# Projections of a two-layer conditioned transformer kernel in three fp32r products instead of plain fp32, with the second conditioning streamed among the weights and a new order

## The chip, the cores and the metric

The kernel runs on one core of one Trainium2 chip. The metric is the device time of one execution in microseconds (us), median of the runs shown. TensorE (PE) multiplies matrices, its weight loads are shown apart (PEld); VectorE is DVE, ScalarE is ACT, GpSimd is POOL, and SyncE (SP) issues all the DMAs here. Each engine works through its own list of instructions in order and waits on semaphores for the others.

## What is computed

Two transformer layers over x (4 sequences of 512 rows, 256 channels, 16 heads of 16 channels), each conditioned by cond_1024. Cut to what matters:

```python
# layer 0
ada = silu(cond) @ ada_w.T + ada_b                  # six vectors of 256 per sequence
h = ln(x) * (1 + s1) + sh1
q, k, v = split(h @ qkv_w.T + qkv_b)                # rope on q and k
attn = softmax(q k^T / 4);  o = attn @ v
x = x + (o @ proj_w.T + proj_b) * g1
h2 = ln(x) * (1 + s2) + sh2
x = x + (gelu(h2 @ fc1_w.T + fc1_b) @ fc2_w.T + fc2_b) * g2
# layer 1: the same with rmsnorm and a gated MLP, conditioned by a small network
t = swiglu(cond @ w_t1 + b_t1) @ w_t2 + b_t2
h = rmsnorm(x) * g1 * (1 + scale1) + shift1;  x = x + mha(h)
h = rmsnorm(x) * g2 * (1 + scale2) + shift2;  x = x + (a * silu(gate)) @ w_fo + b_fo
```

All of it is in fp32. The tolerance is that of fp32, so a product in the faster type fp32r, which keeps fewer bits of its operands, is only good enough if the operands are split in a high and a low part.

## The kernel before

A unit is one sequence in one layer; there are 8 (`UNITS`), worked through one behind the other, four of layer 0 and then four of layer 1. A unit's 16 heads go in four quads of four heads, 32 quads in all. The work of a quad: `peaks` (scores with queries on the partitions, of which DVE takes the row maximum), `top` (the maxima are turned and go by DMA into the operand), `scores` (keys on the partitions, with the maximum subtracted inside the product), the exponential on ACT (L1428), `values` (L920) and `output`. Beside the quads of unit u run the projection and MLP of unit u-1 (`post_pieces`) and the norm, query, key and value projection of unit u+1 (`pre_pieces`).

The order is written out by hand: each piece of work has a tick in the tables `FIRST_AT`, `PRE_AT`, `POST_AT`, `SPLIT_AT`, `LOAD_AT`, `QUAD_AT` (a quad is 112 ticks, `SQ`, a unit 448), all pieces are sorted by tick, and each engine issues its own in that order. PSUM has eight banks: `ps_o` for the values, `ps_b` for the MLP's second product, and a ring of six that all other products share; each use gets the bank whose last reader comes first in the order.

What the change touches:

- `q_and_k` (L858): one output chunk of 128 query or key channels for 512 rows, two products (k = 0, 1) with plain fp32 weights `wf` and rows `hf`. `v` (L871) and `project` (L959): one tile of 128 rows against 256 channels, two products. An fp32 product shows in the trace as two matmul instructions.
- `hf` holds the rows of the first norm (h1), then of the attention output (o), then of the second norm (h2), so each writer waits for the last reader of the one before. ACT writes it in `modulated` (L1383) and `channels` (L1452).
- The MLP is already in three products: DVE rounds h2 to `hh` (L1230), POOL subtracts to get `hl` (L1565), and `up` (L989) multiplies high by low, low by high, high by high. Its weights come in chunks of 128x512 by `load_w`, through three staging places in `mlp`; ACT rounds each (`split_w`, L1485) and DVE subtracts (L1269). `down` (L1006) does the same with the hidden values.
- Rope: ACT takes q and k out of PSUM into `raw` (`take`, L1399), DVE and POOL multiply and add into `turned`, ACT rounds it to `high` (L1409), POOL subtracts to get `low` (L1542), SP spills both to DRAM (L792, L795), and `fill` (L807) reads them back in the layout of the quads.
- Layer 1's conditioning: `t1` and `t2` come whole (0.5 and 1 MB) into places that are used later, and `net_1` (L1032) and `net_2` (L1047) multiply in the first stage, before and between the first peaks.
- The bias of v is added by DVE in `take_v` (L1141).

## Time and profile before

| | us |
|---|---|
| median of 3 runs | 815.72 |
| runs | 815.72, 809.18, 816.38 |
| the profiled execution, its own time | 818.03 |
| its span, first to last instruction | 816.1 |
| PE busy | 769.3 |
| DVE busy | 632.6 |
| ACT busy | 491.0 |
| POOL busy | 290.6 |
| mean granted TensorE clock | 0.962 |

The sums of busy time overlap between engines. A matmul's row shows its own duration, which for neighbours in the pipeline overlaps; the time that a matmul takes of PE is the distance to the start of the next.

### The profile page before, as it was taken

The numbers are of one execution on the slowest core, as the hardware profiler recorded it, in microseconds if no ns is written. First come the engines' busy times: TensorE is split into PE (matmuls) and PEld (weight loads), VectorE is DVE, ScalarE is ACT, GpSimd is POOL, SyncE is SP. The second block draws the span as 40 slices with busy tenths as digits, with TensorE's granted clock in tenths as the row PEclk, the third lists the DMA queues.
The fourth block names the chain that finished last, engine by engine and source line by source line (L and its number), as shares of the span: only waits on it lengthen the run. The fifth ranks groups of instructions, "written<-read, shape, count | busy, mean of one in ns | idle before, by whom it ended". The sixth has DMA issues, their size and how long they took to land.

```text
span 816.1 us, 14249 instructions
## 1 busy us (share of the span) xinstructions
PE 769.3 (94%) x4800; PEld 485.8 (60%) x4800; DVE 632.6 (78%) x1349; ACT 491.0 (60%) x1015; POOL 290.6 (36%) x263
## 2 busy tenths in 40 slices
PE   4999999999999999999999999999999999999496
PEld 3654334466645765566646664668547685776396
DVE  3377898879887897879888999978878879753354
ACT  1114785777657875587758777674666656556132
POOL 0321204534354526334364335332343223222334
PEclk9776999999999999899999999999999999999799
DMA  8475645511234015414322515630254212000000
GB/s 323 130 208 155 191 121 143 155 40 41 84 102 136 14 32 150 135 40 143 79 85 60 144 52 143 183 92 1 65 143 126 57 40 67 2 1 27 1 2 27
DMA packets 34153, 76.27 MB, mean 93 GB/s; under 512 B 4512, under 2 KB 9248, under 8 KB 33824
## 3 DMA queue, kind: packets, MB, share of 16 engines
q1 hardware_dynamic: 34080, 75.35, 32.7%
q8 instruction: 39, 0.64, 0.3%
q14 instruction: 34, 0.28, 0.1%
HBM read 39.42 MB, written 35.65 MB: 92 GB/s over the span
## 4 chain that ended last, share of the span: by engine, by line
PE 72%; DVE 13%; POOL 4%; issue 3%; DMA 3%; ACT 2%; SPq 1%; POOLq 0%; ACTq 0%; DVEq 0%
PE ring L989 17%; PE ps_o L920 11%; PE ps_b L1006 10%; PE ring L893 8%; DVE top L1178 7%; PE ring L906 7%; PE ring L858 7%; PE ring L871 3%; PE ring L959 3%; DMA qt<-top_t 2%; PE ring L931 1%; POOL sines L1531 1%; PE ring L840 1%; POOL hl L1565 1%; PE ring L1020 1%
## 5 line engine op out<-in xcount | busy, mean ns | idle before, releaser
L1178 DVE TENSOR_REDUCE top<-ring 128x1 f32<-128x512 f32 x512 | 321.5, 683 | 42.3 <-PE ring L906 40.7
L1428 ACT ACTIVATE pr<-ring 128x512 f32<-128x512 f32 x512 | 270.2, 605 | 67.0 <-PE ring L893 62.9
L1572 POOL TENSOR_TENSOR act_l<-mlp,act_h 128x256 fp32r<-128x256 f32 x128 | 101.7, 795 | 248.0 <-DVE act_h L1255 248.0
L920 PE MATMUL ps_o<-pr,va 128*17 128x512 f32 x1024 | 133.9, 606 | 0.2 <-ACT pr L1428 0.2
L906 PE MATMUL ring<-kt,qt 48*128 48x512 f32 x512 | 123.3, 459 | 4.5 <-ACT pr L1428 1.3
L893 PE MATMUL ring<-qt,kt 49*128 49x512 f32 x512 | 117.5, 455 | 4.7 <-DMA qt<-top_t 4.2
L1465 ACT ACTIVATE mlp<-ring,col 128x256 f32<-128x256 f32 x128 | 61.1, 477 | 85.5 <-PE ring L989 57.5
L893 PEld LDWEIGHTS ring<-qt,kt 49*128 49x128 f32 x512 | 51.9, 185 | 76.2 <-issue 51.5
L906 PEld LDWEIGHTS ring<-kt,qt 48*128 48x128 f32 x512 | 56.4, 190 | 68.7 <-issue 38.6
L989 PE MATMUL ring<-hh,wl 128*128 128x256 f32 x384 | 83.5, 300 | 6.0 <-issue 3.5
L989 PE MATMUL ring<-hh,wh 128*128 128x256 f32 x384 | 79.4, 289 | 0.0
L989 PE MATMUL ring<-hl,wh 128*128 128x256 f32 x384 | 79.3, 289 | 0.0
L1241 DVE SCALAR_TENSOR_TENSOR mlp<-mlp 128x256 f32<-128x256 f32 x128 | 58.3, 455 | 26.5 <-ACT mlp L1472 24.9
L1006 PE MATMUL ps_b<-wh,act_l 128*128 128x256 f32 x256 | 78.0, 305 | 0.9 <-POOL act_l L1572 0.8
L989 PEld LDWEIGHTS ring<-hh,wl 128*128 128x128 f32 x384 | 61.0, 196 | 22.0 <-issue 12.2
L1006 PE MATMUL ps_b<-wl,act_h 128*128 128x256 f32 x256 | 72.3, 282 | 0.0
L1006 PE MATMUL ps_b<-wh,act_h 128*128 128x256 f32 x256 | 72.2, 282 | 0.0
L1531 POOL TENSOR_TENSOR sines<-raw,trig 128x1024 f32<-128x1024 f32 x16 | 44.1, 2758 | 77.5 <-issue 45.9
L858 PE MATMUL ring<-hf,wf 128*128 128x512 f32 x128 | 67.9, 673 | 1.3 <-ACT hf L1383 1.3
L989 PEld LDWEIGHTS ring<-hh,wh 128*128 128x128 f32 x384 | 62.0, 199 | 0.0
L989 PEld LDWEIGHTS ring<-hl,wh 128*128 128x128 f32 x384 | 61.7, 198 | 0.0
L1561 POOL TENSOR_TENSOR xs<-xs,add 128x512 f32<-128x512 f32 x32 | 40.9, 1280 | 55.2 <-DVE add L1216 53.8
(86 smaller groups left out, 1035.0 us busy)
## 6 DMA issues: line engine op xcount, KB each, us to landing
scratch<-high SPq DMA_DIRECT2D x48, 512.0 KB, 5.1
qt<-scratch SPq DMA_DIRECT2D x64, 192.0 KB, 3.5
kt<-scratch SPq DMA_DIRECT2D x64, 192.0 KB, 4.4
scratch<-low SPq DMA_DIRECT2D x16, 512.0 KB, 5.9
mlp<-in_w_split SPq DMA_DIRECT2D x20, 256.0 KB, 3.5
xs<-in_x SPq DMA_DIRECT2D x4, 512.0 KB, 5.1
out_x<-xs SPq DMA_DIRECT2D x4, 512.0 KB, 2.9
pr<-in_w_ada SPq DMA_DIRECT2D x2, 512.0 KB, 6.3
```

What stands on the lines that cost most here:

```text
L858: last = nc.tensor.matmul(bank[:, :], w[:, k, c * P:(c + 1) * P], hf[:, k, :], start=(k == 0), stop=(k == KC - 1))
L893: nc.tensor.matmul(bank[:, :], kt[r:r + SHIFT + 1, n % NSLOT, h // 2, t * P:(t + 1) * P], qt[r:r + SHIFT + 1, n % NSLOT, h // 2, :], start ...
L906: nc.tensor.matmul(bank[:, :], qt[r:r + SHIFT, n % NSLOT, h // 2, t * P:(t + 1) * P], kt[r:r + SHIFT, n % NSLOT, h // 2, :], start=True, s ...
L920: last = nc.tensor.matmul(ps_o[32 * h:32 * h + HD + 1, :], va[:, u % 2, t, QUAD * g + h, :], pr[:, slot, :], start=(t == 0), stop=(t == T ...
L989: last = nc.tensor.matmul(bank[:, s * TH:(s + 1) * TH], wp[:, k, c:c + P], hp[:, k, half * TH:(half + 1) * TH], start=(n == 0), stop=(n == ...
L1006: last = nc.tensor.matmul(ps_b[:, s * C:(s + 1) * C], ap[:, at % 2, s * P:(s + 1) * P], wp[:, f, :], start=(f == 0 and s == 0 and n == 0), ...
L1178: nc.vector.tensor_reduce(top[:, n % 2, c:c + 1], bank[:, :], AX_X, ALU.max, negate=True).then_inc(free, 1)
L1241: step(nc.vector.scalar_tensor_tensor(val[at % 2], aux[at % 2], 1.0, val[at % 2], ALU.add, ALU.mult))
L1428: nc.scalar.activation(pr[:, at % NP, :], bank[:, :], ACT.Exp, scale=SCALE).then_inc(free, 1)
L1465: nc.scalar.activation(val[at % 2], src, ACT.Identity, bias=col[:, c:c + 1]).then_inc(val_in, 1)
L1531: nc.gpsimd.tensor_tensor(sines[:, :, :], raw[:, :, :], trig[:, 1, :].unsqueeze(1).to_broadcast([P, 2, L]), ALU.mult).then_inc(sin_in, 1)
L1572: nc.gpsimd.tensor_tensor(act_l[:, at % 2, :], src, act_h[:, at % 2, :].bitcast(F32), ALU.subtract).then_inc(act_l_in, 1)
```

## The change

- The query, key, value and output projections are done in three fp32r products: weights in a high and a low part (`qh`, `ql`), rows in `hh` and `hl`. Each output takes 6 matmul instructions in place of 4.
- ACT writes the high part itself and then the plain value: two activations per 128x512 where there was one, in `modulated` and `channels`. The subtraction is `rest` on POOL, for h1, o and h2 (on DVE for the very first unit). DVE's rounding of h2 goes. h2 has its own `hh2` and `hl2`, so the waits between h1, o and h2 are others.
- Four chunks of layer 0's projection weights come first through the staging places and are split; layer 1's four come late (`late_load`, `split_late`) through one place of their own.
- Layer 1's conditioning weights come as six chunks through the same staging places, between the projection chunks and the MLP's; `net_1` and `net_2` are moved behind the first scores.
- The bias of v is added in `channels` instead of `take_v`, which becomes a copy.
- `high` and `low` of the rope are written over `raw` and `sines`. So `take` and `sine` of the next pair wait until the spill of the last has landed; before, only `high` and `low` waited for it.
- All the tables of ticks are new.

```diff
-                    for k in range(KC):
-                        last = nc.tensor.matmul(bank[:, :], w[:, k, c * P:(c + 1) * P], hf[:, k, :],
-                                                start=(k == 0), stop=(k == KC - 1))
+                    for wp, hp in ((ql, hh), (qh, hh), (qh, hl)):
+                        for k in range(KC):
+                            if wp is ql:
+                                pe.wait_ge(hh_in, whole("h1", u) - KC + k + 1)
+                            elif hp is hl:
+                                pe.wait_ge(hl_in, whole("h1", u) - KC + k + 1)
+                            last = nc.tensor.matmul(bank[:, :], wp[:, i, k, at:at + P], hp[:, k, :],
+                                                    start=(n == 0), stop=(n == 3 * KC - 1))
...
+                    for hp, wp in ((hh, ql), (hl, qh), (hh, qh)):
+                        for k in range(KC):
+                            last = nc.tensor.matmul(bank[:, 0:C], hp[:, k, t * P:(t + 1) * P], wp[:, V_CHUNK, k, :],
...
+                    for hp, wp in ((hh, ql), (hh, qh), (hl, qh)):
+                        if hp is hl:
+                            pe.wait_ge(hl_in, whole("o", u))
+                        for k in range(KC):
+                            last = nc.tensor.matmul(bank[:, s * C:(s + 1) * C], hp[:, k, t * P:(t + 1) * P],
...
                 def modulated(u, n, k):
...
+                    if k == 0:
+                        for free in rows_free(name, u) + staged_free(name, u):
+                            ac.wait_ge(*free)
+                    nc.scalar.activation(high_of(name)[:, k, :], bank[:, :], ACT.Identity, bias=bias, scale=scale).then_inc(hh_in, 1)
+                    nc.scalar.activation(hf[:, k, :], bank[:, :], ACT.Identity, bias=bias, scale=scale
+                                         ).then_inc(emptied_in, 1)
...
                 def channels(u, k):
...
+                    nc.scalar.activation(hh[:, k, :], bank[:, :], ACT.Identity, bias=col[:, b:b + 1]).then_inc(hh_in, 1)
+                    nc.scalar.activation(hf[:, k, :], bank[:, :], ACT.Identity, bias=col[:, b:b + 1]).then_inc(emptied_in, 1)
...
+                def rest(u, name, k):
+
+                    gp.wait_ge(hh_in, whole(name, u) - KC + k + 1)
+                    gp.wait_ge(*emptied(name, u, k))
+                    nc.gpsimd.tensor_tensor(low_of(name)[:, k, :], hf[:, k, :], high_of(name)[:, k, :].bitcast(F32),
+                                            ALU.subtract).then_inc(hl_in, 1)
...
-                def split_h(u, k):
...
-                    nc.vector.tensor_copy(hh[:, k, :], hf[:, k, :]).then_inc(hh_in, 1)
...
                 def take(u, c):
...
                     if half == 0 and at:
 
-                        ac.wait_ge(cos_in, at)
-                        ac.wait_ge(sin_in, at)
+                        ac.wait_ge(low_in, at)
+                        ac.wait_ge(*spill_landed((at - 1) // 2, (at - 1) % 2))
...
                 def load_w(c):
 
+                    last = c - NSTAGE
+                    if last >= 0 and is_net(last):
+                        sp.wait_ge(*filled(*net_use(last)))
+                    elif last >= 0:
+                        sp.wait_ge(wl_in, splits_before(last) + 1)
...
+                def late_load(c):
+
+                    if c == 0:
+                        sp.wait_ge(*emptied("gates", B - 1))
+                    else:
+
+                        sp.wait_ge(late_l_in, c)
+                    sp.dma_start(late[:, :], w_qkv[:, (NQKV + c) * CHUNK:(NQKV + c + 1) * CHUNK]).then_inc(late_in, 16)
```

Of the tables, the stage before the first peaks. PE before: mod_0(0), norm_turn, qk 0 and 1, v 0 and 1, qk 2, net_1, v 2, mod_0(1), qk 3, two parts of net_2, v 3, gates 0 to 3, two more parts of net_2, peaks. PE after: mod_0(0), norm_turn, qk 0 and 1, gates 0, v 0, gates 1, mod_0(1), qk 2, gates 2, v 1, qk 3, v 2 and 3, peaks. On SP, the load of x1 stood between the first spill and the first fill and stands ahead of the spill now. In the rest of the kernel, the order of the quads and of the MLP stays nearly as it was.

## Rows read from the trace of the kernel before

**Rows 1.** The page: busy time of each engine, share of the span, instructions.

```profile
PE 769.3 (94%) x4800; PEld 485.8 (60%) x4800; DVE 632.6 (78%) x1349; ACT 491.0 (60%) x1015; POOL 290.6 (36%) x263
```

**Rows 2.** Busy time by stretch: length, engines with instructions, clock, DMA share, GB/s.

```profile
200.00:300.00 100.00, 98.40 (x628) 59.61 (x626) 85.20 (x189) 71.92 (x155) 42.80 (x38) 0.98 0.27 76
...
400.00:500.00 100.00, 97.81 (x607) 59.58 (x604) 90.97 (x196) 70.89 (x150) 47.41 (x41) 1.00 0.33 92
```

**Rows 3.** The chain that ended last: shares by engine, then by line.

```profile
PE 72%; DVE 13%; POOL 4%; issue 3%; DMA 3%; ACT 2%; SPq 1%; POOLq 0%; ACTq 0%; DVEq 0%
```

```profile
by line: PE ring L989 17.0%; PE ps_o L920 10.7%; PE ps_b L1006 10.2%; PE ring L893 7.9%; DVE top L1178 7.4%; PE ring L906 7.4%; PE ring L858 6.9%; issue 3.5%; PE ring L871 3.2%; PE ring L959 2.7%; DMA qt<-top_t 2.0%; PE ring L931 1.5%; POOL
```

**Rows 4.** Pieces of that chain: start us, length us, what, instructions.

```profile
228.69 3.63 PE ring L858 x8
232.99 1.92 PE ring L871 x8
...
326.59 3.43 PE ring L858 x8
```

**Rows 5.** Timeline of PE inside the MLP, full clock: start us, us, instruction.

```profile
299.92 0.28 PE L1006 MATMUL ps_b<-wh,act_l 128*128 128x256 f32 x1
...
300.04 0.28 PE L1006 MATMUL ps_b<-wl,act_h 128*128 128x256 f32 x1
```

**Rows 6.** PE's groups by line: count | busy us, mean ns | idle before, releaser.

```profile
L858 PE MATMUL ring<-hf,wf 128*128 128x512 f32 x128 | 67.9, 673 | 1.3 <-ACT hf L1383 1.3
L871 PE MATMUL ring<-wf,hf 128*128 128x256 f32 x128 | 33.9, 407 | 1.0 <-DVE va L1141 0.9
L959 PE MATMUL ring<-wf,hf 128*128 128x256 f32 x128 | 31.5, 390 | 1.3 <-ACT hf L1452 0.8 <-DVE top L1178 0.2
```

**Rows 7.** ACT's groups by line, same columns.

```profile
L1428 ACT ACTIVATE pr<-ring 128x512 f32<-128x512 f32 x512 | 270.2, 605 | 67.0 <-PE ring L893 62.9 <-PE ps_o L920 2.9
...
L1383 ACT ACTIVATE hf<-ring,mod 128x512 f32<-128x512 f32 x32 | 24.1, 782 | 38.6 <-PE ring L840 38.5
...
L1485 ACT ACTIVATE wh<-mlp 128x512 fp32r<-128x512 f32 x20 | 12.7, 635 | 5.2 <-DMA mlp<-in_w_split 5.2
```

**Rows 8.** Groups of POOL (whole span) and DVE (100 to 760 us), same columns.

```profile
L1565 POOL TENSOR_TENSOR hl<-hf,hh 128x512 fp32r<-128x512 f32 x16 | 23.4, 1473 | 24.1 <-DVE hh L1230 24.1
```

```profile
L1269 DVE SCALAR_TENSOR_TENSOR wl<-mlp,wh 128x512 fp32r<-128x512 f32 x14 | 11.7, 837 | 0.1
...
L1230 DVE CAST hh<-hf 128x512 fp32r<-128x512 f32 x14 | 5.7, 434 | 0.2 <-ACT hf L1383 0.2
```

**Rows 9.** The chain through the first stage, in order of time.

```profile
17.36 6.52 PE ring L858 x8
...
42.18 7.61 PE ring L1020 x16
...
50.57 0.44 PE ring L906
```

**Rows 10.** SP's issue of the first fill, and landing times of the fill's DMAs.

```profile
40.24 1.31 SPq L807 DMA_DIRECT2D qt<-scratch  x2
```

```profile
DMA to landing us min/median/max: 3.8/5.1/6.3
```

**Rows 11.** Timeline in the last unit: DVE's rounding alone, POOL, DVE's rounding beside it.

```profile
768.86 0.43 DVE L1230 CAST hh<-hf 128x512 fp32r<-128x512 f32 x1 [2.08 <-ACT hf L1383]
769.36 1.26 POOL L1565 TENSOR_TENSOR hl<-hf,hh 128x512 fp32r<-128x512 f32 x1 [3.76 <-DVE hh L1230]
769.65 1.26 DVE L1230 CAST hh<-hf 128x512 fp32r<-128x512 f32 x1 [0.37 <-ACT hf L1383]
```

**Rows 12.** One rope pair of unit 4, and the landing time of its low part's spill.

```profile
420.75 1.05 ACT L1409 ACTIVATE high<-turned 128x1024 fp32r<-128x1024 f32 x1
...
423.31 2.37 POOL L1542 TENSOR_TENSOR low<-turned,high 128x1024 fp32r<-128x1024 f32 x1
```

```profile
DMA to landing us min/median/max: 4.9/4.9/4.9
```

More of the change, by code:

```diff
@@ L546 @@
         USES.append(("proj", args[0], args[1] // 2))
-    elif kind == "net_2":
-        USES += [("net_2",)] * (args[0] == 0)
-    elif kind in ("qk", "v", "up", "top", "gates", "net_1", "mod_0"):
+    elif kind in ("qk", "v", "up", "top", "gates", "net_1", "net_2", "mod_0"):
         USES.append((kind, *args))
@@ L821, in store @@
                     sp.dma_start(out_v[j], xs[:, j]).then_inc(x_out, 16)
-                whole_program("sp", {"load": load, "load_w": load_w, "spill": spill, "fill": fill, "top": top_row,
+                whole_program("sp", {"load": load, "load_w": load_w, "late": late_load, "spill": spill, "fill": fill, "top": top_row,
                                      "store": store})
@@ L1603, in prologue @@
     s_ada = [name(f"ada{i}") for i in range(3)]
-    s_wf = [name(f"wf{i}") for i in range(3)]
     fill = name("fill")
```

941 lines of the change are left out of this document (514 added, 427 removed).

## The prediction

> **What bounds the kernel now.** I read the page's busy shares first: PE is busy 94% of the span, DVE 78%, ACT 60%, POOL 36% [rows 1]. Then the busy time in stretches of 100 us, since the shares are averages over a first stage, a long even middle and a tail: in the middle DVE reaches 85 and 91 of 100 us beside a PE at 98, with ACT at 71 [rows 2]. Then the chain that ended last, which tells how much of each engine's work the end really waited for: 72% of the span is PE, 13% DVE, 2% ACT [rows 3]. So PE sets the time, and DVE is close behind it. A shorter PE helps at nearly its full worth only as long as DVE follows.
>
> A busy PE is not a PE at its peak, so I priced PE by distances between starts. Eight fp32 instructions of 512 columns take 3.43 us when their neighbours are of the same kind, 0.429 each; 3.63 when a neighbour is fp32r, so one change of kind on each side costs about 0.1 us. Eight of 256 columns take 1.92, less 0.2 for the changes, 0.215 each [rows 4]. In the MLP, fp32r instructions of 256 columns start 0.12 us apart [rows 5].
>
> **PE's part.** Query and key: 8 units x 4 chunks x 2 k x 2 = 128 instructions before [rows 6], 128 x 0.429 = 54.9 us. After, 8 x 4 x 6 = 192 of fp32r with 512 columns over all 128 rows, which the trace doesn't have. From below they cost half of a 512 fp32 instruction, 0.215 (an fp32 instruction seems to stream its columns twice: 0.215 at 256, 0.429 at 512); from above twice the 256-column one, 0.24. I take the middle, 0.227: 43.6 us, so 11.3 less (bounds 8.8 and 13.6). Value and output projection: 128 + 128 instructions [rows 6] at 0.215 = 55.0; after, 2 x 8 x 4 x 6 = 384 at 0.12 = 46.1: 8.9 less. Sorting both sets of tables, neighbouring pieces on PE change between fp32 and fp32r 399 times before and 363 times after: 36 x 0.1 = 3.6 less. At the start TensorE's clock is at its lower level, 1.2 GHz: the first 8 query and key instructions take 6.52 us [rows 9], twice their price. They cost 8 x 0.429 = 3.4 us extra, the 12 that replace them 12 x 0.213 = 2.6: 0.9 less. Sum: 25 us less PE time.
>
> Not all of it reaches the end. The chain holds 6.9 + 3.2 + 2.7 = 12.8% of 816.1, 104 us, of these three lines [rows 3], against 133 us of their busy time [rows 6]: 78%. 0.78 x 25 = 19.3: **19 us gained**.
>
> **The first stage.** Before, the first fill is issued at 40.24 us; SP issues two DMAs in 1.31 us, so its four in 2.6, and they need 3.8 to 6.3 us from issue to landing [rows 10], so the data is there at about 47. The first peaks start at 50.57, because PE works through all four gates and parts of net_2 ahead of them [rows 9]. After, those parts and the last of the gates are behind the peaks (gates are 7.61 us for four): 3.5 us gained. The load of x1 is no more between spill and fill, one issue, 0.65 us. The first two chunks at half clock take 12 x 0.427 = 5.1 us for 6.52, but the second high part is now the third activation, 0.8 later: 0.6. The new chunk splits run on ACT and DVE while PE is still on mod_0 and the first norm, so I cost them nothing; if the first chunk landed late, each us of that would show in full in front of qk, up to the 4 to 6 that a DMA takes to land [rows 10]. Net_1 and net_2 don't vanish, they fill PE slots later. In sum **5 us gained**, from 0 to 9.
>
> **ACT's part.** 32 more activations in modulated at 0.782 us and 16 in channels at between 0.605 and 0.782, and 8 splits of projection chunks at 0.635 [rows 7]: 25 + 11 + 5 = 41 us, 491 to 532. By ACT's 2% of the chain [rows 3], 16 us for 491 busy, that would be 1.4 us. But the second high part of every h1 comes one activation (0.78) later, with all the scores queued behind it: 8 x 0.78 = 6 if PE had nothing else, and it mostly has. **2 us lost**, from 0 to 7. The cover is ACT's slack: at 71.9 of 100 us now [rows 2], it gets 5.1 more per unit of 88 us, some 81%. If that cover is gone, the exponentials are late, then values, and PE with it.
>
> **DVE's part.** It loses 16 roundings at 0.434 = 6.9, gains 8 chunk subtractions at 0.837 = 6.7 [rows 8]. take_v as a copy out of PSUM costs between its old price and a quarter less; I take nothing. Two rests in the first unit lie in its idle start. **0**.
>
> **POOL's part.** 46 rests in place of 16 subtractions, 30 more at 1.26 to 1.47 us [rows 8, 11] = 38 to 44 us. POOL is at 36%, so nothing is lost by queueing, but v and the third query product now wait for it; behind PE's peaks and scores of other quads that is hidden. If it were not, it would be 2.5 us per unit. What POOL does to DVE is a rival below.
>
> **The spill wait.** take of the second pair now waits on ACT until the first pair's spill has landed, with the exponentials queued behind it. In unit 4 that is 1.05 for high, 2.4 for low [rows 12], 0.4 to get into SP, 4.9 to land [rows 12]: 7.7 us from the end of high. Between high and that take the new order gives ACT 5.4 us of work in unit 4 (eight exponentials at 0.605 [rows 7] and an output copy) and 7 to 9.8 in the other units past the first, waits not counted. So the spill is just covered: **1 us lost**. If it isn't covered the kernel pays, see below.
>
> **Sum.** 818.0 (the profiled execution's own time, 1.9 more than its span) - 19.3 - 5 + 2 + 1 = 796.7. The median of the runs, 815.7, is 2.3 below that execution: 794.4, say **795 us**.
>
> **Rivals.**
>
> *More is gained.* DVE and ACT waits for PE shrink too, all 25 us arrive, the first stage gives 9, ACT costs nothing, the new 512-column product is at 0.215 (2 more): 815.7 - 36 = 780. For: in the middle ACT's exponentials wait 63 us for PE [rows 7]. Against: DVE at 85 to 91 of 100.
>
> *DVE takes the gain back through POOL.* In the last unit DVE's rounding takes 0.43 us alone and 1.26 beside a subtraction on POOL [rows 11]. Each of 30 more POOL subtractions can hold a DVE instruction 0.83 us: up to 25 us more DVE work. In the middle DVE has about 15 of 100 us left, and with the period 3% shorter and this on top it would stand at 92, above anything in the trace, so most of PE's gain would turn into waits for the row maxima: 4 of 19 left, the first stage's 5 kept, ACT's and the spill's 3 lost: 815.7 - 6 = 810. Against it: most of DVE's time is the row maximum out of PSUM, and the roundings of h2, which stood right beside POOL, are gone.
>
> The Trainium skill has this as a rule (GPSIMD Engine Reference, section 1, Specifications): POOL's SBUF interfaces are shared with VectorE, with contention for DVE instructions in a two-port mode or with two SBUF inputs. The trace agrees, 0.43 against 1.26 us. It speaks against this change: by the row's full price on every new subtraction the sum above would be 810, by none of it 795.
>
> *Slower: the spill wait is not covered.* If SP is late with the spill (it stands behind fills and tops, which wait themselves) and landing takes 6.3 us, the longest of the first fill [rows 10], rather than 4.9, ACT stands still some 5 us in each of 7 units with the exponentials behind: 35 us more, 830. It decides from about 3 us per unit on, where it eats all of the 21 us net gain. For: SP has every DMA in one queue, and load_w of the conditioning chunks now waits on net_1 and net_2 in it. Against: the order leaves 7 to 10 us in most units.
>
> *The products are not cheaper.* If a 512-column fp32r instruction with full weights cost 0.29 or more, query and key alone would gain nothing (192 x 0.286 = 54.9). Then PE saves 13.7, of which 10.7 arrive: 804, near the bound of no change. The 0.12 at 256 columns with full 128x128 weights speaks against it.
>
> **How the numbers follow.** A measurement of this kernel can tell about 1% from no change, 8 us: faster is below 807.6, slower above 823.9. The forecast (784 to 804) has 0.50, more gained (below 784) 0.18, products not cheaper 0.05, DVE takes it back (805 to 818) 0.17, spill wait (above 820) 0.10. Faster: 0.50 + 0.18 + 0.05 and a third of 0.17 = 0.78. Same 0.13, slower 0.09. The range cuts 0.1 off at each end: 775 to 813.
>
> **What would show it.** Right: the 512-column products start 0.22 to 0.24 us apart, the three projection lines take some 105 us of busy PE in place of 133, the first peaks start at 44 to 47 us, DVE stands at about 88 of 100 in the middle. Wrong: ACT idle before take with a DMA of the spill as releaser, above 1 us per unit; DVE's busy sum above 645; peaks and scores with longer waits for DVE; or a granted clock in the middle well below the 0.98 to 1.00 of before [rows 2].

## The result and the profile after

The changed kernel is slower. Its median is 839.42 us beside 813.26 us for the kernel before, a ratio of 1.031 (95% interval 1.027 to 1.035), so about 26 us are lost. The prediction had 795 us and a range up to 813. One execution each of e5, e8 and e14 was disturbed (2.2 to 3.2 ms; in e5 and e8 the profiled one): the medians below count it, the ratios, the clocks and the views don't.

The page of the kernel after, its busy shares and then its chain, answers to [rows 1, 3]:

```profile
PE 772.6 (92%) x4992; PEld 506.3 (60%) x4992; DVE 642.8 (77%) x1344; ACT 527.6 (63%) x1071; POOL 334.1 (40%) x293
...
PE 70%; DVE 7%; DMA 7%; ACT 4%; POOL 4%; issue 4%; SPq 2%; POOLq 0%; ACTq 0%; DVEq 0%
PE ring L1146 18%; PE ps_b L1163 11%; PE ps_o L1077 11%; PE ring L1050 9%; PE ring L1063 8%; PE ring L1012 5%; DVE top L1331 4%; POOL sines L1683 3%; DMA scratch<-sines 3%; PE ring L1115 3%; PE ring L1088 2%; DMA kt<-scratch 1%; SPq L940 1%; ACT hh L1533 1%; PE ring L1027 1%
```

PE was to get 25 us shorter and its busy time rose by 3. DVE's share of the chain fell from 13% to 7%. What grew is DMA (3% to 7%) and ACT (2% to 4%). The spill of the rope's low part, "scratch<-sines", is new among the lines.

Of the signs that the prediction named, its projection lines take 120.6 us of busy PE for 133.3, not 105, and DVE stands at 84 of 100 in the middle, not 88. ACT's wait for the spill came (13.0 us, 1.6 a unit), DVE's sum stayed under 645, and the clock in the middle fell, as the rows below show.

Where the time is lost is seen best from unit to unit. PE's timeline has the first values instruction of unit 0 and of unit 1, in the kernel before:

```profile
76.85 0.62 PE L920 MATMUL ps_o<-pr,va 128*17 128x512 f32 x4
137.65 0.62 PE L920 MATMUL ps_o<-pr,va 128*17 128x512 f32 x4
```

and after:

```profile
65.43 0.62 PE L1077 MATMUL ps_o<-pr,va 128*17 128x512 f32 x4
143.22 0.62 PE L1077 MATMUL ps_o<-pr,va 128*17 128x512 f32 x4
```

The kernel after starts its values 11.4 us earlier and is 5.6 us late one unit on: the quads of unit 0 took 60.8 us before and 77.8 after. Read in the same way, the next six units take 89.3, 88.2, 80.3, 88.8, 95.5 and 97.1 us before and 93.3, 92.1, 81.3, 90.4, 99.7 and 94.7 after, 12 us more together, and the rest up to the end of the span 139.2 and 143.7. So the loss is spread over the whole kernel: -11.4 + 17.0 + 12.3 + 4.5 = 22.4 us, which is the difference of the spans (838.5 - 816.1).

Busy time by stretch, kernel before first and then after (length, then PE, PEld, DVE, ACT, POOL with their instructions, clock, DMA share, GB/s). The first line of each is the stretch between those two values instructions, the second is the middle:

```profile
77.00:138.00 61.00, 57.62 (x330) 25.07 (x326) 55.95 (x103) 46.20 (x90) 10.08 (x8) 1.00 0.56 154
...
100.00:700.00 600.00, 588.26 (x3769) 358.97 (x3766) 515.93 (x1087) 409.23 (x852) 232.48 (x204) 0.99 0.34 91
```

```profile
65.00:143.00 78.00, 72.26 (x400) 36.26 (x397) 59.72 (x115) 50.87 (x98) 13.28 (x9) 0.82 0.57 158
...
100.00:700.00 600.00, 581.30 (x3786) 368.05 (x3786) 502.78 (x1040) 424.99 (x869) 265.46 (x223) 0.96 0.34 92
```

Beside the quads of unit 0 the granted clock was 1.00 before and 0.82 after, and PE has 14.6 us more busy time there. In the middle the kernel after gives PE 581 us of work in 600 where it was 588. Over the whole span the mean clock is 0.940 for 0.962. A mean m over a span s means 2 x (1 - m) x s at 1.2 GHz, the rest at 2.4 GHz: 101 us after and 62 before. Work at half rate costs PE half of that time, so the 39 us more are worth up to 20 of the 22 us between the two spans, if PE is what the rest waits for. This is an estimate, and it doesn't say whether the clock is a cause of its own or follows from what PE does in the new kernel.

### The profile page after: what moved, and what is told of

Same layout as the page of the kernel before. It is cut to its first block, busy times and chain, and to the rows that moved or that the text cites. A ratio compares the mean times of both kernels' runs of the same rounds, so it can differ in the third digit from the quotient of the medians.

```text
span 838.5 us, 14781 instructions
## 1 busy us (share of the span) xinstructions
PE 772.6 (92%) x4992; PEld 506.3 (60%) x4992; DVE 642.8 (77%) x1344; ACT 527.6 (63%) x1071; POOL 334.1 (40%) x293
## 4 chain that ended last, share of the span: by engine, by line
PE 70%; DVE 7%; DMA 7%; ACT 4%; POOL 4%; issue 4%; SPq 2%; POOLq 0%; ACTq 0%; DVEq 0%
PE ring L1146 18%; PE ps_b L1163 11%; PE ps_o L1077 11%; PE ring L1050 9%; PE ring L1063 8%; PE ring L1012 5%; DVE top L1331 4%; POOL sines L1683 3%; DMA scratch<-sines 3%; PE ring L1115 3%; PE ring L1088 2%; DMA kt<-scratch 1%; SPq L940 1%; ACT hh L1533 1%; PE ring L1027 1%
## 5 line engine op out<-in xcount | busy, mean ns | idle before, releaser
L1063 PE MATMUL ring<-kt,qt 48*128 48x512 f32 x512 | 128.0, 463 | 21.2 <-DMA kt<-scratch 12.0
L1077 PE MATMUL ps_o<-pr,va 128*17 128x512 f32 x1024 | 138.2, 623 | 0.6 <-ACT ot L1584 0.3
L1050 PE MATMUL ring<-qt,kt 49*128 49x512 f32 x512 | 125.3, 478 | 6.4 <-DMA qt<-top_t 1.9
L1063 PEld LDWEIGHTS ring<-kt,qt 48*128 48x128 f32 x512 | 58.7, 194 | 83.1 <-issue 43.8
L1716 POOL TENSOR_TENSOR hl<-hf,hh 128x512 fp32r<-128x512 f32 x46 | 58.8, 1290 | 59.5 <-ACT hf L1534 36.1
L1163 PE MATMUL ps_b<-wh,act_l 128*128 128x256 f32 x256 | 77.8, 304 | 0.9 <-POOL act_l L1723 0.7
L1683 POOL TENSOR_TENSOR sines<-raw,trig 128x1024 f32<-128x1024 f32 x16 | 51.5, 3221 | 64.2 <-ACT raw L1550 64.2
L1163 PEld LDWEIGHTS ps_b<-wh,act_l 128*128 128x128 f32 x256 | 48.8, 190 | 17.2 <-issue 16.1
```

What stands on the lines that cost most here:

```text
L1050: nc.tensor.matmul(bank[:, :], kt[r:r + SHIFT + 1, n % NSLOT, h // 2, t * P:(t + 1) * P], qt[r:r + SHIFT + 1, n % NSLOT, h // 2, :], start ...
L1063: nc.tensor.matmul(bank[:, :], qt[r:r + SHIFT, n % NSLOT, h // 2, t * P:(t + 1) * P], kt[r:r + SHIFT, n % NSLOT, h // 2, :], start=True, s ...
L1077: last = nc.tensor.matmul(ps_o[32 * h:32 * h + HD + 1, :], va[:, u % 2, t, QUAD * g + h, :], pr[:, slot, :], start=(t == 0), stop=(t == T ...
L1163: last = nc.tensor.matmul(ps_b[:, s * C:(s + 1) * C], ap[:, at % 2, s * P:(s + 1) * P], wp[:, f, :], start=(f == 0 and s == 0 and n == 0), ...
L1683: nc.gpsimd.tensor_tensor(sines[:, :, :], raw[:, :, :], trig[:, 1, :].unsqueeze(1).to_broadcast([P, 2, L]), ALU.mult).then_inc(sin_in, 1)
L1716: nc.gpsimd.tensor_tensor(low_of(name)[:, k, :], hf[:, k, :], high_of(name)[:, k, :].bitcast(F32), ALU.subtract).then_inc(hl_in, 1)
```

## The experiments

All ratios are to the kernel before, run on the same chip beside each experiment, with the 95% interval behind them. e1, e2, e5, e7, e8 and e12 are built from the kernel before and keep its order and its tables of ticks. e3, e4, e6, e9, e10, e11, e13 and e14 are built from the kernel after, each a step away from the last.

**e1: the products alone.** The kernel before, with three F32R products from one small tile of weights.

```diff
-                    for k in range(KC):
-                        last = nc.tensor.matmul(bank[:, :], w[:, k, c * P:(c + 1) * P], hf[:, k, :],
-                                                start=(k == 0), stop=(k == KC - 1))
+                    for n in range(3):
+                        for k in range(KC):
+                            last = nc.tensor.matmul(bank[:, :], dw[:, c % 2 * P:(c % 2 + 1) * P], hf[:, k, :],
+                                                    start=(n == 0 and k == 0), stop=(n == 2 and k == KC - 1))
```

> The kernel before, with its order and its buffers, in which only the products of the query, key, value and output projections are changed: six fp32r instructions in place of four fp32 ones. The rows are rounded to fp32r as they are written, the weights are one rounded tile of the same sizes, and the same product is made three times, so the projections' values are not the reference's; no second activation, no subtraction, no split of weights is added. It measures the first term of the forecast by itself. If PE's term was right: PE's stream some 25 us shorter and about 19 us of it at the end, 813 becomes 794, with 512-column instructions 0.22 to 0.24 us apart. Rival (DVE is the real bound of the middle, PE only follows it): PE waits longer in front of peaks and scores instead, 806 to 813.

Measured: 818.33 against 812.26 us, 1.007 (1.004 to 1.010). With cheaper products alone this kernel is no faster; it is 6 us slower. Summing the distances between starts on PE, the three projections went from 134.4 to 114.7 us, the 20 that the two instruction prices gave (11.3 + 8.9 of the 25). But peaks grew by 5.3 us, scores by 7.3 and values by 5.8, with nothing changed in them. PE's idle time before scores and peaks went from 9.2 to 18.5 us, and 11.8 us of it now end with DVE:

```profile
L913 PE MATMUL ring<-kt,qt 48*128 48x512 f32 x512 | 125.8, 470 | 7.5 <-DVE va L1150 3.5 <-DMA kt<-scratch 2.3 <-ACT pr L1441 0.7
L900 PE MATMUL ring<-qt,kt 49*128 49x512 f32 x512 | 120.2, 463 | 11.0 <-DVE va L1150 4.3 <-DVE top L1187 4.0 <-DMA qt<-top_t 1.9
```

The middle:

```profile
100.00:700.00 600.00, 577.01 (x3899) 372.77 (x3892) 521.95 (x1078) 404.83 (x843) 229.18 (x205) 0.97 0.32 89
```

PE stands at 577 of 600 where it was 588, at a clock of 0.97 where it was 0.99, and DVE has 522 where it had 516. The mean clock over the whole is 0.949 for 0.962: 83 us at the lower level in place of 62 (83 for 55 as medians over all runs of both).

**e2: ACT's extra activations alone.** The kernel before, where every activation of modulated and channels is done once more, into a tile that nobody reads.

```diff
+                    hx_settled()
+                    twice(nc.scalar.activation(hx[:, :], bank[:, :], ACT.Identity, bias=mod[:, j, term:term + 1],
+                                               scale=mod[:, j, factor:factor + 1]))
                     nc.scalar.activation(hf[:, k, :], bank[:, :], ACT.Identity, bias=mod[:, j, term:term + 1],
```

> The kernel before with its order, in which ACT does each activation of modulated and of channels twice, 48 more, the first time into a tile that nobody reads (the gates of two sequences share a place for want of room, so layer 0's gates are not the reference's). It measures what ACT's second activations cost by themselves, without POOL, DVE or the spill. By the forecast's step: 35 us more ACT work, 2 us at the end, 815. Rival (ACT's queue is as tight as PE's, each late h1 and o is paid for by the exponentials and products behind it): 0.6 to 0.8 us for each of the 24 stages where PE waits for the rows, up to 35 us in all, 825 to 845, and longer stretches at TensorE's lower clock.

Measured: 839.06 against 812.26 us, 1.033 (1.029 to 1.036): 27 us more. ACT's groups show what was added (count | busy us, mean ns | idle before, releaser):

```profile
L1397 ACT ACTIVATE hx<-ring,mod 128x512 f32<-128x512 f32 x32 | 25.1, 785 | 42.2 <-PE ring L842 22.5 <-PE ring L961 11.3 <-issue 8.4
...
L1469 ACT ACTIVATE hx<-ring 128x512 f32<-128x512 f32 x16 | 9.6, 601 | 13.5 <-PE ring L944 11.9 <-issue 1.7
```

So 34.7 us of work went to an engine that is busy 60% of the span and holds 2% of the chain, and three quarters of it arrived at the end. Between the two profiled executions, 20 us apart, the mean clock is nearly the same (0.959 for 0.962), so most of it isn't the clock. Over all runs it is 0.957 for 0.966, some 18 us more at 1.2 GHz, which can be up to 9 of the 27.

**e5: the same activations behind the rows.** As e2, but both extra ones of a block come after the two that the products wait for. They read a tile in SBUF, of the same size, in place of the bank.

```diff
                     nc.scalar.activation(hf[:, k, :], bank[:, :], ACT.Identity, bias=mod[:, j, term:term + 1],
                                          scale=mod[:, j, factor:factor + 1]).then_inc(free, 1)
+                    if k == KC - 1:
+                        ac.wait_ge(*emptied(name, u, 0))
+                        again(bank, func=ACT.Identity, bias=mod[:, j, term:term + 1],
+                              scale=mod[:, j, factor:factor + 1])
```

> The kernel before with the same number of additional activations of the same size as in e2, but all of them behind the two that write the rows, reading and writing tiles that nothing waits for. ACT's work is that of e2 (e2's was 27 us slower than before), only the rows are not delayed. (The gates of two sequences share a place, so layer 0's gates are not the reference's.) Theory A, the delay of the rows costs (PE stands in front of the projections and of up): most of the 27 us goes, 812 to 820. Theory B, ACT's queue costs (the exponentials stand behind the additional work, and PE behind them): it stays, 830 to 840.

Measured: 831.27 against 815.39 us, 1.020 (1.016 to 1.024). Some 16 us of e2's 27 stay when the rows are no later than before: what stands behind the extra work on ACT, the exponentials above all, is then what pays. The other 11, by the difference, are the delay of the rows themselves.

**e3 and e4: the spill wait.** e3 is the kernel after with some space freed: the bias of the output rows is read from a tile that is there anyway, and the gates of four conditionings share two places, so those values aren't the reference's. It is the control. e4 is e3 with the high and low parts in tiles of their own again, so that take and sine don't wait for the spill.

```diff
-                        ac.wait_ge(low_in, at)
-                        ac.wait_ge(*spill_landed((at - 1) // 2, (at - 1) % 2))
+                        ac.wait_ge(cos_in, at)
+                        ac.wait_ge(sin_in, at)
...
-                    nc.scalar.activation(raw[:, :, :].bitcast(F32R), turned[:, :, :], ACT.Copy).then_inc(high_in, 1)
+                    if at:
+                        ac.wait_ge(*spill_landed((at - 1) // 2, (at - 1) % 2))
+                    nc.scalar.activation(high[:, :, :], turned[:, :, :], ACT.Copy).then_inc(high_in, 1)
```

> The changed kernel with room made in SBUF for the next one: the projections' row biases are read from another tile and not loaded, and the gates of sequences 0 and 2, and of 1 and 3, share a place, so the residuals are not the reference's. Nothing waits otherwise than in the changed kernel. Every theory: within 1% of the changed kernel, 835 to 843; it is what the next one is to be compared with.

> The kernel of e3_after_room with the rope's high and low parts in tiles of their own again, as in the kernel before, so that take and sine of the next pair no longer wait for the landing of the last pair's spill; order and all else as in the changed kernel. If that wait is the cause (theory: some 3 us a unit, in ACT's queue in front of the exponentials, and the lower clock that follows PE's idle stretches): 839 becomes 805 to 820. If the cause is the second activation and POOL's share in the path of the rows, or the order: 832 or more.

Measured: e3 835.93 us, 1.029 (1.025 to 1.033), as the kernel after. e4 830.57, 1.022 (1.016 to 1.027). The best value for the wait is 5.4 us; the two intervals overlap, so the size is loose, but the trace carries it. This is the chain of the kernel after around the first spill of unit 3 (start us, length us, what):

```profile
248.12 1.07 ACT raw L1557
...
249.88 0.60 SPq L940
250.48 0.04 issue
250.52 1.48 SPq L940
252.00 0.04 issue
252.05 7.09 DMA scratch<-sines
259.16 0.04 ACTq L1548
259.20 0.05 issue
259.25 1.27 ACT raw L1550 x2
```

The low part landed after 7.1 us and take followed at once: the end waited for the DMA. ACT's group for take, kernel after and then e4:

```profile
L1550 ACT ACTIVATE raw<-ring,col 128x512 f32<-128x512 f32 x32 | 21.4, 686 | 34.9 <-PE ring L1012 21.8 <-DMA scratch<-sines 13.0
```

```profile
L1549 ACT ACTIVATE raw<-ring,col 128x512 f32<-128x512 f32 x32 | 21.7, 689 | 24.8 <-PE ring L1013 24.8
```

The DMA is gone as a releaser, 13 us in five waits, and with it less than half of that from the time.

**e6: the second activation.** e4 with the second activation of each block cut to one column; the low parts are then zero.

```diff
-                    nc.scalar.activation(hf[:, k, :], bank[:, :], ACT.Identity, bias=bias, scale=scale
+                    nc.scalar.activation(hf[:, k, 0:1], bank[:, 0:1], ACT.Identity, bias=bias, scale=scale
```

> The kernel of e4_after_own_tiles (830.6) with the second activation of modulated and channels cut to one column; the low part is then the difference of the high part with itself, so the projections and the MLP's first product lack their low parts. POOL's subtractions stay. If the second activations cost in the changed kernel what they cost in the kernel before: 27 us less, 803 to 808. If the changed kernel's order hides them, and its own order or POOL's share is what costs: 822 to 830.

Measured: 823.75 against 815.39 us, 1.011 (1.007 to 1.015), against 1.022 for e4. So 1% or some 8.5 us by the ratios went with what was cut. But the cut took only part of the work away. These are the second activations in the kernel after and then in e6:

```profile
L1534 ACT ACTIVATE hf<-ring,mod 128x512 f32<-128x512 f32 x32 | 25.0, 782 | 0.0
L1595 ACT ACTIVATE hf<-ring,col 128x512 f32<-128x512 f32 x16 | 11.1, 693 | 0.0
```

```profile
L1533 ACT ACTIVATE hf<-ring,mod 128x1 f32<-128x1 f32 x32 | 11.3, 354 | 0.0
L1596 ACT ACTIVATE hf<-ring,col 128x1 f32<-128x1 f32 x16 | 4.3, 267 | 0.0
```

An activation of one column still takes 0.27 to 0.35 us. So 8.5 us is the price of 20.5 us of ACT's work, and 15.6 of the 36.1 us stay in e6 and in all kernels built from it (e9, e10, e11, e13, e14).

**e7 and e8: a lighter DVE.** e7 is the kernel before with the row maxima over half their width, and the scale of the exponentials cut so that nothing overflows. e8 is e7 with the products of e1.

```diff
-                nc.vector.tensor_reduce(top[:, n % 2, c:c + 1], bank[:, :],
+                nc.vector.tensor_reduce(top[:, n % 2, c:c + 1], bank[:, 0:L // 2],
```

> The kernel before with the row maxima taken over half of the columns, which takes some 0.27 us off each of DVE's 512 reductions, 137 us in all (the maxima are then wrong, and the exponential's scale is made tiny to keep it finite, so attention is not the reference's). Theory of the forecast, PE sets the time and DVE only follows: 0 to 15 us less. Theory that DVE sets the middle as much as PE does: 25 to 60 us less.

> The kernels of e7_light_max and e1_products in one: half-width maxima, and the projections in six fp32r instructions (values as told for both). It is compared with e7. If e1's lack of a gain came from DVE, which gave PE no time back, the products now gain what PE's stream lost, 12 to 20 us under e7. If it came from TensorE's clock, which falls as soon as PE has gaps: within 5 us of e7, with more time at the lower level.

Measured: e7 805.03 us, 0.987 (0.983 to 0.992); e8 799.88, 0.980 (0.976 to 0.985). DVE's busy sum fell from 632.6 to 512.9 us, by 120 (137 were expected), and that is worth 10 us, so DVE alone isn't the bound. But with it out of the way the same products take 5 us off instead of adding 6 (the intervals of e7 and e8 just overlap).

**e9, e10, e11: what is left.** e9 is e6 with POOL's subtractions for h1 and o cut to one column. e10 is e9 with the projections as plain fp32 products of the high parts, all waits kept, though the one for the low part now stands ahead of the first product (2.8 us of PE's idle time in its trace). e11 is e10 without loading the second conditioning's weights (its products read the identity matrix), so no chunk on SP's queue waits for them.

In this order:

```diff
+                    n = L if name == "h2" else 1
+                    nc.gpsimd.tensor_tensor(low_of(name)[:, k, 0:n], high_of(name)[:, k, 0:n].bitcast(F32), high_of(name)[:, k, 0:n].bitcast(F32),
                                             ALU.subtract).then_inc(hl_in, 1)
```

```diff
-                    for wp, hp in ((ql, hh), (qh, hh), (qh, hl)):
...
+                        last = nc.tensor.matmul(bank[:, :], qh[:, i, k, at:at + P].bitcast(F32), hh[:, k, :].bitcast(F32),
+                                                start=(k == 0), stop=(k == KC - 1))
```

```diff
+                    if is_net(c):
+                        return
-                    if last >= 0 and is_net(last):
-                        sp.wait_ge(*filled(*net_use(last)))
```

> The kernel after with high and low in tiles of their own, the second activation of a block cut to one column (as in e6_one_activation), and now POOL's subtractions for h1 and o cut to one column too (L columns are left out, only those of h2 stay whole). What is left of the change: the products in three parts, the streamed weights, the new order. First theory: POOL hides the subtractions, the 1.1% that e6 is above the kernel before come from the order and the streaming: e9 is within 2 us of e6, ratio 1.010. Rival, POOL's subtractions slow DVE where they lie beside it: about 26 of them at 1.29 us are gone, DVE's instructions beside them ran up to three times as long, so DVE loses up to 26 us of its time and the ratio is 1.000 or below.

> e9 with the products in plain fp32 again (one product of the high parts instead of three, all waits kept): what is left of the change is the new order and the streamed weights. TensorE's stream grows by about 20 us against e9. First theory, the products are worth little or less than nothing at this kernel's balance because the readers of the six banks set the pace and a lighter TensorE falls to 1.2 GHz more often (e1: 6 us slower with the cheap products, e8: 6 us faster): e10 is within 6 us of e9, ratio between 1.00 and 1.02, and its time at the lower clock is less than e9's. Rival, the products do pay as soon as the other engines are relieved, 78% of 20 us as the prediction had it: e10 is 15 us slower than e9, ratio about 1.03.

> e10 without the stream of the second conditioning's weights: the six chunks are not loaded, and its products read the identity instead, so that no load of a weight chunk waits for these products. First theory, these waits on SP's queue and the six chunks ahead of the MLP's weights are what made the quads of unit 0 take 77.8 us in the kernel after instead of 60.9: e11 is 8 to 15 us faster than e10, and the distance from the first values of unit 0 to those of unit 1 falls to 65 us or less. Rival, it is the fuller engines of the first stage (the clock, the moved splits): e11 is within 3 us of e10.

Measured: e9 825.84 against 810.41 us, 1.017 (1.010 to 1.025). e10 842.16, 1.039 (1.031 to 1.046). e11 838.50, 1.032 (1.026 to 1.039). Three things follow. POOL's 30 extra subtractions cost nothing that can be measured; e9 isn't below e6. In this order the products are worth 16 us (e10 to e9, the intervals don't touch), with the opposite sign to e1; the rival of e10's expectation was right. And e10, with the projections as costly as before, is 32 us above the kernel before. What it still has of the change is the new order and tables, the weights streamed and split inside it, and the 15.6 us of one-column activations: together they are far from free. The middle of e10:

```profile
100.00:700.00 600.00, 585.53 (x3621) 350.74 (x3621) 501.87 (x1036) 407.44 (x865) 230.91 (x224) 0.97 0.33 92
```

PE runs 3621 instructions in this stretch where the kernel before, with the same 4800 in all, runs 3769. The mean clock of this execution over the whole is 0.962, as before, and it is 19 us longer by the spans: that much isn't the clock. It is one of e10's two fastest, though. Over all runs e10 has 0.956 for 0.967, some 21 us more at 1.2 GHz, so up to 10 of the 32 can be the clock. e11 is not clearly faster than e10, and its stretch from unit 0's values to unit 1's is 73.6 us for 74.4: the stream of the second conditioning is not the cause. My first theory for it fell.

**e12: the new work in the old order.** e1 and e2 together, on the kernel before.

> The kernel before with both: the projections' products in three F32R products on one weight tile (not the weights of the reference) as in e1, and every activation of the modulated and channel blocks twice as in e2; order and tables of before. First theory, the new order is what the new work needs: in the order of before the two costs add up, 1.0069 and 1.0325 give 1.039 or more, so the kernel after (1.031) is the better order for this work. Rival, the new order is worse for any work: the products relieve what the activations load, and the ratio is 1.025 or below, under that of the kernel after.

Measured: 834.42 against 812.05 us, 1.024 (1.017 to 1.031). It lies below e2 (1.033), so with ACT loaded the products gain a little in the old order too, 5 us by the medians and 7 by the ratios; the intervals just overlap. And it is level with e4 (1.022), which does this work and also POOL's subtractions and the weight splits, without the spill wait. So the new order isn't worse for the work it was written for. For e10 there is no such pair: the kernel before has neither its one-column activations nor its splits.

**e13: the splits beside unit 0.** e9 with the twelve MLP chunks of unit 0 split in one column only; POOL clears these weights at the start instead.

```diff
-                    nc.scalar.activation(hi, stage[c % NSTAGE], ACT.Copy, scale=chunk_factor(c)).then_inc(wh_in, 1)
+                    few = FIRST_MLP <= c < FIRST_MLP + NPLACE
+                    n = 1 if few else CHUNK
+                    nc.scalar.activation(hi[:, 0:n], stage[c % NSTAGE][:, 0:n], ACT.Copy, scale=chunk_factor(c)).then_inc(wh_in, 1)
```

> e9 with the twelve MLP weight chunks of unit 0 split only in one column on ACT and DVE (the tiles are cleared by POOL at the start instead, so these weights are zero): about 10 us of ACT and 10 us of DVE less, most of them beside the quads of unit 0. First theory, the splits moved beside the quads make their engines late there: the distance from the first values of unit 0 to those of unit 1 falls from 74.5 us to 67 or less, and the time by 5 to 8 us, ratio 1.008. Rival, it is the second conditioning's own products and the lower clock in this stretch: the distance stays above 71 us and the time within 3 us of e9.

Measured: 825.11 us, 1.013 (1.006 to 1.020). The time is that of e9. The stretch did shrink, from 74.5 to 68.7 us, but POOL's clearing made the first peaks 5.6 us and the first values 7.7 us later, and unit 1's values come at 140.0 us for 138.2. The run is inconclusive on its question. What it does show is that a first stage 8 us later is caught up by the next unit.

**e14: a lighter DVE in the new order.** e9 with the row maxima of e7.

> e9 with the row maxima over half their width (the softmax's shift is another, the exponentials' scale is cut), which takes about 137 us from DVE, as e7 did to the kernel before for 10 us less. First theory, the new order lives off the same margins as the old: 8 to 12 us less than e9, ratio 1.003 to 1.007. Rival, DVE bounds the new order where it did not the old: 20 us less or more, ratio 0.992 or below.

Measured: 810.17 us, 0.994 (0.989 to 0.998), 16 us less than e9 by the medians and 19 by the ratios, where e7 gave 10. The size lies between both theories. DVE matters somewhat more in the new order, and is still not the one bound: 137 us less by the expectation (119 by the busy sums) for 16 to 19.

## Why the prediction was wrong

**The prices of PE's work were right.** The projections' distances fell by 20 us in e1. This is the chain of the kernel after, around unit 4:

```profile
323.21 4.04 PE ring L1115 x24
...
331.63 2.98 PE ring L1012 x12
...
414.00 3.10 PE ring L1115 x24
```

2.98 us for twelve products of 512 columns is 0.248 each with the changes of kind in it; the forecast was 0.227 and 0.1 a change. 3.10 us for twenty-four of 256 columns is 0.129. The rival "the products are not cheaper" is out. In the kernel after, the same lines still take 120.6 us of busy PE: 41 us of their time is at 1.2 GHz, where it was 18 before.

**The step that failed first is the 78%.** The prediction turned the share of these lines in the chain [rows 3] over their busy time [rows 6] into a rate at which a shorter PE reaches the end: 19 us gained. What 20 us of PE are worth depends on what else is in the program. The same cheaper products gave:

| where | us at 1.2 GHz, profiled execution | the same, median of the runs | effect on the time |
| --- | --- | --- | --- |
| order before (e1) | 62 to 83 | 55 to 83 | +6 us |
| order before, DVE light (e7 to e8) | e8's is disturbed | 51 to 65 | -5 us |
| order before, ACT loaded (e2 to e12) | 69 to 105 | 73 to 102 | -5 to -7 us |
| order after (e10 to e9) | 63 to 76 | 74 to 77 | -16 us |

Two things eat it. One is the clock: in the three pairs in the old order it falls more where PE gets lighter. By the medians 28, 14 and 29 us more at 1.2 GHz cost PE up to half of that, 14, 7 and 14 us, if PE is what the rest waits for. In the new order they differ by 3, within the spread of the runs, and there 16 of the 20 us arrive, as the 78% had it. (The profiled execution of e10 is one of its fastest, so the first column overstates that pair.) Taken off the 20 us, the clock leaves -6, -13, -6 and -18, which is what e12 and e9 measured within 3 us; e1 and e8 are 12 and 8 us above it. The prediction named a clock "well below" that of before among the signs of being wrong and gave it no term. No run holds the clock, so whether it is a cause or follows from the waits stays open.

The other is that scores and peaks got longer without being changed (7 and 5 us in e1), since they use the banks that DVE and ACT empty. The trace of e1 shows the wait, 11.8 us before them that end with DVE's copy of v and its row maxima, of the size of the 12 us that the clock leaves over; and relieving DVE turned +6 into -5. DVE at 85 and 91 of 100 [rows 2] was read as "close behind", but the sum priced it at nothing.

**ACT's term was mis-sized by far: 2 us forecast, with 0 to 7 as bounds.** In the old order it is 27 us for 34.7 us of work (e2), in the new one about 8.5 for the 20.5 that e6 took away (e4 to e6). Products and activations together, in the old order, were forecast at 17 us gained and cost 19 to 22 (e12), which is most of the 26 us lost. The forecast took ACT's 2% of the chain for its price. An engine that idles 40% in short pieces can still be late each time: a block's two extra activations are 1.6 us in front of the exponentials queued behind it. e5 leaves 16 of the 27 to this queue. The prediction saw "all the scores queued behind it" and wrote that PE mostly has other work; it has not. Its cover was also misreckoned: 5.1 us on the 71.9 of 100 in a unit of 88 make 78 of 100, not 81. Measured was 71 (425 of 600 us), so ACT's share gave no warning.

**The spill wait: 1 us forecast, 5.4 measured.** It needed 7.7 us between high and take: 2.8 until the low part is issued and 4.9 to land [rows 12]. In unit 3 the high part ended at 249.19 (248.12 + 1.07) and the low part was issued at 252.05, 2.9 us later, as forecast. But it took 7.1 us to land: 10 us in all, beyond the cover of 7 to 10 us that the order gives. The 4.9 was one landing out of 16, and among the shorter ones. All 16 of the low part, kernel before and then after:

```profile
DMA to landing us min/median/max: 3.7/5.9/7.0
```

```profile
DMA to landing us min/median/max: 3.7/6.0/7.5
```

With the median and 2.8 the wait is 8.7 us and already past the cover in some units. The rival mechanism was the right one, at a seventh of its price: 35 us would have needed a stall in every unit, and there were five waits of 13 us in all.

**The first stage was right and was given back.** First peaks at 44.83 us for 50.57, in the 44 to 47 that were forecast. PE stood idle for 10.0 us ahead of them until the fill landed:

```profile
39.43 5.27 DMA kt<-scratch
44.83 4.13 PE ring L1063 x10
...
65.50 0.98 PE ps_o L1077 x8
66.48 0.43 PE ring L1063 x2
66.91 0.24 PE ring L1050 x2
67.14 1.88 PE ring L1191 x16
```

The last line is net_1, now between peaks and scores. "Net_1 and net_2 don't vanish, they fill PE slots later" was written and no price put to it. In this stretch before, PE ran at 1.00 and peaks at full rate; there were no free slots to fill. The moved conditioning costs PE 6.1 us there by the distances between starts, the splits more work for ACT and DVE (11 and 10 of them for 8 and 8), and the clock of 0.82 means 28 us at 1.2 GHz, up to 14 us. That is more than the 17 us by which the stretch grew.

Part of the lower clock stands right behind the moved products. These are net_1 and the two parts of net_2 in the kernel after, and then the stretches at 1.2 GHz:

```profile
67.08 1.95 PE L1191 MATMUL ring<-small,mlp 128*128 128x4 f32 x16
77.76 1.95 PE L1206 MATMUL ring<-small,mlp 128*128 128x4 f32 x16
92.16 2.38 PE L1206 MATMUL ring<-small,mlp 128*128 128x4 f32 x16
```

```profile
69.40:72.80 3.40, 3.40 (x17) 1.16 (x14) 2.54 (x6) 2.77 (x6) 1.13 (x1) 0.50 0.50 130
79.60:83.00 3.40, 3.40 (x15) 1.01 (x15) 2.53 (x7) 1.15 (x3) 0.00 (x0) 0.50 0.98 330
93.30:100.10 6.80, 6.80 (x31) 3.37 (x30) 5.43 (x11) 2.69 (x6) 0.00 (x0) 0.50 0.34 84
```

Each of the three is followed by a fall, and so were net_1 and the large part of net_2 in the kernel before (they end at 29.0 and 52.8 us, the clock falls at 29.9 and 53.8). It isn't so every time: in e10 the clock stays up behind net_1, in e13 behind the last part. These 13.6 us at half rate cost PE up to 7, which with the 6.1 of the products makes 13 of the 17 us, by estimate. The runs don't settle it: without the conditioning's stream, but with its products (e11), the stretch was as long; without the splits (e13) it was shorter, but from a later start. The products alone weren't taken out.

**The order had no term at all.** The sum treated the change as a list of edits to a kernel whose order stays. The largest single entry is what e10 leaves, 32 us, and the order is only a part of it. Its 15.6 us of one-column activations would be 6.5 us at the price of e6 and 12 at that of e2, so 20 to 26 us are left for the order, the streaming and the splits, by estimate. It is not that the new order is bad; for its own work it is level with the old one (e4 and e12). My reading, which no run shows, is that an order of this kind is fitted to the lengths of its pieces, and that e10 took pieces out of their fit, as e1, e2 and e12 did from the other side. The parts don't add up in the way in which the prediction added them: +6 from e1 and +27 from e2 would be 33, and together they are 19 to 22 (e12). A chain that does add up, by construction, goes through the kernel after in ratios: order, streaming, splits and one-column activations with plain products +3.9%, products -2.1, POOL's subtractions -0.6 (nothing, within the intervals), the other columns of the second activation +1.0, spill wait +0.7, space freed +0.2: 3.1%.

**POOL: nothing, as forecast.** e6 and e9 don't tell 30 subtractions from none. The rival "DVE takes it back through POOL" had a price of 25 us of DVE work from [rows 11], and DVE's busy sum is 642.8 for 632.6, 10 more in all. The Trainium skill's rule of shared interfaces (GPSIMD Engine Reference, section 1, Specifications) holds for the pair of instructions in [rows 11]. DVE's main work, the row maximum out of PSUM, doesn't show it: its mean is 682 ns after and was 683 before.

## What to carry to other kernels

The share of an engine in the chain that ended last is no price for work added to it. ACT had 2% of the chain, and 35 us put on it cost 27; look instead at what is queued behind the place where the work goes, and how soon another engine wants it.

Where three engines stand at 98, 88 and 72 of 100, take the relief of the first for nothing until a run shows otherwise, and take an addition to the third at most of its length (27 of 35 us here). Work moved out of a stage with slack is paid where it lands: read the rates of that stretch first, and if PE runs at full rate there, charge all of it.

Edits to a kernel with a fitted order can't be priced one by one. Run one edit in both orders before believing its sign: here the same edit gave +6 and -16 us. The two places differ in ACT's work too, and with ACT loaded the old order gave -5 to -7, so the order is not shown to be the whole reason.

An instruction cut to one column is not gone. Look in the trace at what it still takes before calling its cost measured: here 15.6 of 36.1 us stayed. And compare the clock over all runs, not over the one execution that was profiled.

## What the runs showed of the hardware

TensorE's granted clock fell more when TensorE had less to do, in three pairs of kernels with the same work elsewhere. As medians over the runs the mean clock went from 0.966 to 0.949 (e1), 0.969 to 0.959 (e7 to e8) and 0.957 to 0.939 (e2 to e12). In a fourth, e10 to e9, it stayed within the spread, 0.956 and 0.953. In e1 the engine had pauses just ahead of the falls. These are the stretches before and at two of them:

```profile
243.50:250.30 6.80, 4.96 (x31) 2.40 (x30) 5.82 (x6) 5.01 (x9) 3.38 (x2) 1.00 0.91 301
250.30:257.10 6.80, 6.80 (x30) 4.92 (x31) 6.47 (x14) 4.01 (x9) 2.63 (x2) 0.50 0.00 1
...
411.00:417.50 6.50, 4.13 (x24) 3.19 (x23) 6.40 (x6) 2.96 (x4) 3.78 (x3) 1.00 0.22 46
417.50:424.30 6.80, 4.83 (x17) 1.97 (x18) 5.32 (x10) 1.98 (x4) 1.10 (x1) 0.50 0.72 264
```

PE was busy 4.96 of 6.80 us and 4.13 of 6.50 us, then ran at 1.2 GHz for 6.8 us. In these two places a pause cost more than its own length, since several us of PE at half rate came behind it. It isn't the whole rule: in the kernel before, the fall at 340.50 us comes behind 6.80 us without a gap in PE's busy time:

```profile
333.70:340.50 6.80, 6.80 (x39) 3.33 (x37) 6.07 (x13) 6.01 (x12) 3.06 (x2) 1.00 0.91 295
340.50:347.30 6.80, 6.80 (x28) 3.79 (x27) 5.23 (x10) 2.03 (x5) 1.43 (x2) 0.50 0.05 18
```

Among runs of one and the same kernel the time goes with the clock: the kernel before, run beside e12 to e14, took 809.5 us at a mean clock of 0.967 and 819.1 at 0.955, 9.6 us more for 20 us more at 1.2 GHz.

An activation of 128x1 out of PSUM took 0.27 to 0.35 us, where one of 128x512 took 0.69 to 0.78.

The spill of the low part, 512 KB to DRAM, took between 3.7 and 7.0 us from issue to landing in the kernel before and between 3.7 and 7.5 after, with medians of 5.9 and 6.0. What makes one longer than another wasn't tried.
